# Two transfer queues, a folded scale and filler matmuls in the set-up of an adaLN block with linear attention and experts

## The reference

```python
mod = (silu(c) @ wmod).reshape(2, 6, 1, 256)        # sa, ca, ga, sb, cb, gb
h = layernorm(x) * (1 + ca) + sa
q, k, v = heads(h @ W_qkv)                          # 16 heads of 16
q, k = rope(q), rope(k)
qf, kf = elu(q * 16 ** -0.5) + 1, elu(k) + 1
out = (qf @ (kf.T @ v)) / max(qf @ sum(kf), 1e-6)   # per head
x = x + gate(ga) * (out @ W_out)
h = layernorm(x) * (1 + cb) + sb
x = x + gate(gb) * experts(h)                       # 8 experts, the best 2, capacity 640
```

## Time and profile before

| | us |
|---|---|
| median of 3 runs | 652.75 |
| lowest and highest | 652.57, 653.78 |
| span of the profiled execution | 649.3 |
| around that span, if the execution took the median | 3.45 |
| TensorE, matmuls, busy | 558.4 |
| VectorE, ScalarE, GpSimd busy | 456.7, 318.3, 270.2 |

### The profile page before, as it was taken

The page is one execution under the profiler, slowest core; times in us unless marked ns, Lnnn a source line. Parts: engine busy times, 40 slices in busy tenths (PEclk is TensorE's granted clock), DMA queues, the critical chain, the costliest instruction groups (busy, mean ns, idle before and its releaser), DMA issues.

```text
span 649.3 us, 13329 instructions
## 1 busy us (share of the span) xinstructions
PE 558.4 (86%) x3857; PEld 517.9 (80%) x3857; DVE 456.7 (70%) x1261; ACT 318.3 (49%) x716; POOL 270.2 (42%) x428
## 2 busy tenths in 40 slices
PE   4999889999899510279999999999999999999992
PEld 3677678898777300169999999999999999999992
DVE  3577879998677888877667677577676776666441
ACT  3678768887444410034544544445445444455330
POOL 6588756776678500212107035052070160431221
PEclk9999989999899755579999999999999999999997
DMA  5322258744566560051716627337257175360321
GB/s 164 100 65 69 72 146 257 232 140 142 164 190 194 177 164 1 17 163 34 196 50 124 195 54 156 110 90 158 68 108 209 27 132 160 84 137 10 33 25 16
DMA packets 91910, 75.23 MB, mean 116 GB/s; under 512 B 12108, under 2 KB 88278, under 8 KB 91864
## 3 DMA queue, kind: packets, MB, share of 16 engines
q1 hardware_dynamic: 82872, 58.77, 30.5%
q0 software_dynamic: 8992, 15.90, 13.3%
HBM read 52.48 MB, written 22.16 MB: 115 GB/s over the span
## 4 chain that ended last, share of the span: by engine, by line
PE 57%; DVE 15%; issue 5%; DMA 4%; POOL 2%; ACT 2%; SPq 1%; DVEq 1%; POOLq 0%; ACTq 0%
PE bank L1379 28%; PE bank L1393 14%; PE bank L1414 4%; DVE hit L907 3%; PE bank L1291 2%; PE bank L1428 2%; PE bank L1194 1%; DVE x L870 1%; PE bank L1355 1%; DMA x_in<-x 1%; DMA w_raw<-wd 1%; DVE st L872 1%; PE bank L1336 1%; PE bank L1271 1%; DMA xg<-h_rows,g_idx 1%
## 5 line engine op out<-in xcount | busy, mean ns | idle before, releaser
L508 POOL DMA_INDIRECT xg<-h_rows,g_idx x40 | 44.0, 1100 | 246.3 <-DVE g_idx L1013 236.6
L1379 PE MATMUL bank<-xT_h,w_h 128*128 128x320 f32 x448 | 140.3, 313 | 1.5 <-DVE xT_l L1042 1.0
L1379 PE MATMUL bank<-xT_h,w_l 128*128 128x320 f32 x448 | 138.6, 309 | 0.0
L1379 PE MATMUL bank<-xT_l,w_h 128*128 128x320 f32 x448 | 138.6, 309 | 0.0
L662 ACT CAST hid_h<-hid 128x320 fp32r<-128x320 f32 x112 | 51.5, 460 | 87.6 <-DVE hid L1070 87.6
L518 POOL DMA_INDIRECT out<-yo,s_idx x40 | 67.4, 1685 | 60.7 <-DVE yo L1060 21.9
L1379 PEld LDWEIGHTS bank<-xT_h,w_h 128*128 128x128 f32 x448 | 84.8, 189 | 2.5 <-issue 1.7
L1379 PEld LDWEIGHTS bank<-xT_l,w_h 128*128 128x128 f32 x448 | 84.7, 189 | 0.0
L1379 PEld LDWEIGHTS bank<-xT_h,w_l 128*128 128x128 f32 x448 | 84.6, 189 | 0.0
L658 ACT ACTIVATE act_g<-bank 128x320 f32<-128x320 f32 x112 | 48.9, 437 | 69.4 <-PE bank L1379 68.6
L1075 DVE TENSOR_TENSOR hid_l<-hid,hid_h 128x320 fp32r<-128x320 f32 x112 | 54.8, 489 | 36.6 <-ACT hid_h L662 36.2
(11 more groups left out here) (197 smaller groups left out, 1276.9 us busy)
## 6 DMA issues: line engine op xcount, KB each, us to landing
w_raw<-wg SPq DMA_DIRECT2D x32, 256.0 KB, 3.7
w_raw<-wu SPq DMA_DIRECT2D x32, 256.0 KB, 4.9
w_raw<-wd SPq DMA_DIRECT2D x16, 512.0 KB, 5.9
x_in<-x SPq DMA_DIRECT2D x32, 128.0 KB, 2.1
q_store<-qT SPq DMA_DIRECT2D x32, 128.0 KB, 2.0
q_in<-q_store SPq DMA_DIRECT2D x32, 128.0 KB, 2.1
x_re<-x SPq DMA_DIRECT2D x32, 128.0 KB, 2.1
out<-x SPq DMA_DIRECT2D x32, 128.0 KB, 2.0
```

The costliest lines, as they stand in the source:

```text
L508: nc.gpsimd.indirect_dma_start(out=xg[par][:, a, :], out_offset=None, in_=h2_rows, in_offset=bass.IndirectOffsetOnAxis(ap=g_idx[par][:, a: ...
L1379: last = MM(bank[2 * h + m][:, 0:HCAP], W[i][:, f, at:at + P], XT[j][:, k, cols], start=n == 0, stop=n == 3 * KC - 1)
```

## The change

- SyncE's queue now carries c, the identity alone, x of tiles 0 and 1, the V part of the QKV weights, the rotation table and the other constants. ScalarE's queue carries the modulation weights and the Q and K part, as its first two instructions.
- ScalarE waits for c alone, takes silu, and then the exponential of one number (`warm`), whose result nobody reads.
- The factor 1/4 of Q is taken in ScalarE's rounding and in VectorE's subtraction; the pass over the weights is gone. Rounding and subtraction go in thirds: Q, K, V. The modulation columns are copied behind Q. V is rounded behind tile 0's hT_h and subtracted at the end of step -1. The first product waits for the low parts of Q and K alone, the V product for the third.
- The 90 memsets of `digits` and `swaps` move behind the token loop.
- `keep_warm(n)` multiplies a 128 by 128 tile of ones with itself n times, in bf16, into a bank that nobody has begun to use. TensorE does so 14 times before the transposes of c, 8 times before it waits for the modulation weights, and 24 times before it waits for the low parts ahead of the first product.

The diff, with lines of context left out:

```diff
--- before.py
+++ after.py
@@ -42,6 +42,7 @@
 LAG = TB + 2
+Q_SCALE = float(HD) ** -0.5
 LN_EPS, DEN_EPS, TOPW_EPS, GATE_MIN = 1e-5, 1e-6, 1e-6, 0.25
@@ -174,6 +175,7 @@
         iota_s = sb("iota_s", [P, P], BF16)
+        warm = sb("warm", [1, 1])
@@ -283,6 +285,7 @@
         ld_c, ld_mod, ld_const, ld_w = sem("ld_c"), sem("ld_mod"), sem("ld_const"), sem("ld_w")
+        ld_id, ld_wv, ld_blk = sem("ld_id"), sem("ld_wv"), sem("ld_blk")
         ld_rest, st_mod, ld_ga, ld_all = sem("ld_rest"), sem("st_mod"), sem("ld_ga"), sem("ld_all")
@@ -313,19 +316,21 @@
+        wm = wmod.rearrange("(c p) n -> p c n", p=P)
+        wq = w_qkv.rearrange("(c p) n -> p c n", p=P)
...
         block = ctx.enter_context(nc.Block())
...
             sp.dma_start(c_sb[:, :], c).then_inc(ld_c, 16)
-            sp.dma_start(const_sb[:, :], consts).then_inc(ld_c, 16)
+            sp.dma_start(ident, consts[:, 0:P]).then_inc(ld_id, 16)
             sp.dma_start(x_in[0][:, :], xt[0]).then_inc(ld_x[0], 16)
             sp.dma_start(x_in[1][:, :], xt[1]).then_inc(ld_x[1], 16)
-            wm = wmod.rearrange("(c p) n -> p c n", p=P)
-            sp.dma_start(wmod_sb[:, :, 0:2 * D], wm[:, :, 0:2 * D]).then_inc(ld_mod, 16)
-            sp.dma_start(wqkv_sb[:, :, :], w_qkv.rearrange("(c p) n -> p c n", p=P)).then_inc(ld_w, 16)
+            sp.dma_start(wqkv_sb[:, :, 2 * D:], wq[:, :, 2 * D:]).then_inc(ld_wv, 16)
             sp.dma_start(rope_sb[:, :, :], rope.rearrange("(n p) d -> p n d", p=P)).then_inc(ld_const, 16)
+            sp.dma_start(const_sb[:, P:], consts[:, P:]).then_inc(ld_blk, 16)
@@ -444,13 +449,6 @@
                            allow_small_or_imprecise_dtypes=True).then_inc(plink_s, 1)
-            for n in range(DIGITS):
-                unit = 1 << (TOP_BIT - 1 - 2 * n)
-                for d in range(3):
-                    nc.gpsimd.memset(digits[:, n, d:d + 1], (d + 1) * unit)
-                    ins = nc.gpsimd.memset(swaps[:, n, d:d + 1], (d + 1) * unit | ((d + 1) * unit >> 2))
-            ins.then_inc(plink_s, 1)
...
             def step(s):
@@ -497,7 +495,12 @@
+            for n in range(DIGITS):
+                unit = 1 << (TOP_BIT - 1 - 2 * n)
+                for d in range(3):
+                    nc.gpsimd.memset(digits[:, n, d:d + 1], (d + 1) * unit)
+                    ins = nc.gpsimd.memset(swaps[:, n, d:d + 1], (d + 1) * unit | ((d + 1) * unit >> 2))
+            ins.then_inc(plink_s, 1)
             pool.wait_ge(lgc, NT)
@@ -545,8 +548,12 @@
         def _(act):
-            act.wait_ge(ld_c, 32)
+            act.dma_start(wmod_sb[:, :, 0:2 * D], wm[:, :, 0:2 * D]).then_inc(ld_mod, 16)
+            act.dma_start(wqkv_sb[:, :, 0:2 * D], wq[:, :, 0:2 * D]).then_inc(ld_w, 16)
+            act.wait_ge(ld_c, 16)
             nc.scalar.activation(c_act[:, :], c_sb[:, :], ACT.Silu).then_inc(act_pre, 1)
+            act.wait_ge(plink_s, 1)
+            nc.scalar.activation(warm[:, :], half_neg[0:1, :], ACT.Exp)
@@ -563,13 +570,14 @@
                 if s.rep == -1:
-                    act.wait_ge(dve_pre, 2)
-                    nc.scalar.copy(wqkv_h[:, :, 0:2 * D], wqkv_sb[:, :, 0:2 * D]).then_inc(act_pre, 1)
-                    nc.scalar.copy(wqkv_h[:, :, 2 * D:], wqkv_sb[:, :, 2 * D:]).then_inc(act_pre, 1)
+                    act.wait_ge(ld_w, 16)
+                    nc.scalar.activation(wqkv_h[:, :, 0:D], wqkv_sb[:, :, 0:D], ACT.Copy, scale=Q_SCALE)\
+                        .then_inc(act_pre, 1)
+                    nc.scalar.copy(wqkv_h[:, :, D:2 * D], wqkv_sb[:, :, D:2 * D]).then_inc(act_pre, 1)
                 if on["trh"]:
...
                     if s.rep == -1:
-                        act.wait_ge(dve_pre, 4)
+                        act.wait_ge(dve_pre, 3)
                     wait(act, tr_h, s.t(2))
@@ -585,6 +593,9 @@
                     nc.scalar.copy(hT_h[s.par(1)][:, :, :], hT[:, :, :]).then_inc(hTh_d, 1)
+                if s.rep == -1:
+                    act.wait_ge(ld_wv, 16)
+                    nc.scalar.copy(wqkv_h[:, :, 2 * D:], wqkv_sb[:, :, 2 * D:]).then_inc(act_pre, 1)
                 if on["kv"]:
@@ -712,6 +723,12 @@
+            def w_low(i):
...
+                sl = slice(i * D, (i + 1) * D)
+                dve.wait_ge(act_pre, 2 + i)
+                return V.tensor_tensor(wqkv_l[:, :, sl], wqkv_sb[:, :, sl], wqkv_h[:, :, sl].bitcast(F32), ALU.subtract)
...
             def mod_rows(part):
@@ -720,6 +737,7 @@
                     V.tensor_scalar(mod_row[:, 2, :], row_ps[1][:, 0:D], 1.0, None, ALU.add)
+                    dve.wait_ge(ld_blk, 16)
                     V.tensor_copy(same_e[:, :], same_f)
@@ -782,7 +800,7 @@
                 link(TT(hot1, q, b8(first), ALU.is_equal))
-                dve.wait_ge(act_pre, 4 + part)
+                dve.wait_ge(act_pre, 5 + part)
                 link(V.scalar_tensor_tensor(rest, hot1, -2.0, ex, ALU.mult, ALU.add))
@@ -800,17 +818,11 @@
                 if s.rep == -1:
-                    dve.wait_ge(ld_w, 16)
-                    V.tensor_scalar(wqkv_sb[:, :, 0:D], wqkv_sb[:, :, 0:D], float(HD) ** -0.5, None, ALU.mult)\
-                        .then_inc(dve_pre, 1)
-                if s.rep == -1:
-                    for i, sl in enumerate((slice(0, 2 * D), slice(2 * D, 3 * D))):
-                        dve.wait_ge(act_pre, 2 + i)
-                        ins = V.tensor_tensor(wqkv_l[:, :, sl], wqkv_sb[:, :, sl], wqkv_h[:, :, sl].bitcast(F32),
-                                              ALU.subtract)
-                        if i == 0:
-                            mod_cols()
-                    ins.then_inc(dve_pre, 1)
+                    dve.wait_ge(act_pre, 2)
+                    V.scalar_tensor_tensor(wqkv_l[:, :, 0:D], wqkv_sb[:, :, 0:D], Q_SCALE, wqkv_h[:, :, 0:D].bitcast(F32),
+                                           ALU.mult, ALU.subtract)
+                    mod_cols()
+                    w_low(1).then_inc(dve_pre, 1)
                 if s.rep in (LAG, NT - 4):
@@ -844,6 +856,8 @@
                     finish_stats(mv1, nm1[s.par(3)], ve1[s.par(3)], ag1, stat1, s.t(4))
+                if s.rep == -1:
+                    w_low(2).then_inc(dve_pre, 1)
                 if on["feat"]:
@@ -873,7 +887,7 @@
                 if s.rep == NT + LAG:
-                    dve.wait_ge(plink_s, 13)
+                    dve.wait_ge(plink_s, 12)
                     choose(0, EARLY)
@@ -902,6 +916,7 @@
             link(V.tensor_copy(valT[:, :], bank[0][:, 0:2 * P]))
+            dve.wait_ge(plink_s, 13)
             for n in range(DIGITS):
@@ -1172,11 +1187,20 @@
             PASSES = ((0, 0), (0, 1), (1, 0))
+            def keep_warm(n):
...
+                for _ in range(n):
+                    MM(bank[3][:, 0:P], ones_b[:, :], ones_b[:, :], start=True, stop=True)
...
+            pe.wait_ge(plink_s, 2)
+            keep_warm(14)
             pe.wait_ge(act_pre, 1)
+            pe.wait_ge(ld_id, 16)
             for k in range(KC):
...
             pe.wait_ge(dve_pre, 1)
+            keep_warm(8)
             pe.wait_ge(ld_mod, 16)
@@ -1217,7 +1241,8 @@
                     if s.rep == 0:
-                        pe.wait_ge(dve_pre, 5)
+                        keep_warm(24)
+                        pe.wait_ge(dve_pre, 4)
                     wait(pe, hTl_d, s.t(1))
@@ -1232,6 +1257,8 @@
                     wait(pe, v_done, s.t(0))
+                    if s.rep == 0:
+                        pe.wait_ge(dve_pre, 5)
                     product(v_ps, (hT_h[s.par(0)], hT_l[s.par(0)]), (wqkv_h, wqkv_l), slice(2 * D, 3 * D))\
...
```

## The result

The change made the kernel slower. On one chip the changed kernel took 655.32 us (median of 20 runs, 652.26 to 661.73) beside 653.27 us for the kernel before (20 runs): a ratio of 1.0039, 95% interval 1.0022 to 1.0056. Two more sets on other occasions gave 1.0040 (1.0023 to 1.0057) and 1.0040 (1.0027 to 1.0053). That is 2.0 to 2.7 us lost where I had forecast 1.95 us gained. The single runs scatter by several microseconds, and the long ones show a lower mean granted clock of TensorE (0.941 in the shortest of the 20, 0.931 in the longest), so what follows rests on ratios and on places in the trace that come back in every execution. The changed kernel's profiled execution took 654.88 us, with a span of 652.6.

What follows compares the result with a forecast made beforehand. The prediction took the set-up up to tile 0's first rotation (17.55 us) as what counts, with TensorE busiest at 86%. Rotation at 16.0 gains 1.55, plus 0.4 from the table load: 1.95, so 650.8 us, range 647.7 to 652.9.

Steps and rivals of the forecast that it cites:

- Edits at nothing: Moved memsets fill GpSimd's 2.49 us idle before the reset, pushing it back 0.5; new waits and split constants also cost nothing.
- The 24 ones: On TensorE ahead of the first product: start at 14.1 instead of 11.9, costing 2.2 us at half speed, 0.8 at full.
- near the fast end: First product to rotation of tile 0: 1.9 us taken, between 1.71 at full speed and 3.01 at half.
- my early bound: Earliest landing of the modulation weights on ScalarE's queue: issue at 0.75 plus 4.7 us, so 5.45.
- GpSimd has hn by then: Set-up, before tile 0's transposes end at 9.97: hn is ready because the 90 memsets no longer delay GpSimd's first step.
- the table load at 22.16: ScalarE's 1.28 us load moves to about 3.4 through the small exponential; only about 0.4 us can be gained.
- The second-queue rival: Modulation weights on ScalarE's queue still land at 7.3; only the table load gains, giving 652.2 us; chance 20%.
- the late end: Slow end of the forecast's own range, with landing at 6.8 and product at 3.0 us: 652.4 us.
- The 3.45 us around the span: Median whole time 652.75 lies 3.45 above the profiled span 649.3; the same was added to the new span.
- The early ones: The 14 and 8 ones on TensorE end at 5.5, before the modulation weights land, and cost nothing; 0.5 if weights came at 5.0.
- After it nothing waits for a fixed moment: Behind tile 0's first rotation at 17.55 us: whatever brings that rotation forward comes off the kernel's end.

Runs made afterwards that it cites:

- e8: The changed kernel once more, unchanged, timed against the kernel before: ratio 1.0040.
- e3: The changed kernel without any of the 46 products of ones, memsets still moved: ratio 0.9972 to the kernel before.
- e4: The changed kernel without the products of ones and with the memsets back ahead of GpSimd's token loop: ratio 0.9957, on a second occasion 0.9963.
- e2: The kernel before with only the 90 memsets moved behind GpSimd's token loop: ratio 1.0020, 1.3 us slower.
- e1: The changed kernel with only the 90 memsets put back ahead of GpSimd's token loop: ratio 1.0005 to the kernel before.
- the corners: Four kernels on one chip, f1 to f4: memsets moved or back, 24 ones in or out; the move cost 0.37% with the ones, 0.35% without.
- f1: The changed kernel as it is, with moved memsets and all 46 ones, timed beside f2, f3 and f4: ratio 1.0040.
- f3: The changed kernel without the 24 ones, memsets still moved, the 14 and 8 kept; the 24 ones cost f1 0.23% against it.
- f2: The changed kernel with memsets back ahead of the loop and all 46 ones kept, same program as e1; the move cost f1 0.37% against it.
- f4: The changed kernel with the memsets back and the 24 ones out, the 14 and 8 kept, same program as e6: ratio 0.9982.
- e6: The kernel of e1 without the 24 ones ahead of tile 0's product, the 14 and 8 kept: ratio 0.9982 to the kernel before.
- e7: The kernel of e4 with 46 one-column products of ones added behind TensorE's token loop: ratio 0.9983 to the kernel before.
- e11: The kernel of e1 with the 24 ones replaced by 8 behind tile 0's transposes and 5 behind tile 1's: ratio 0.9951, 646.72 us.
- g1: The kernel of e11 timed once more, unchanged: ratio 0.9939 to the kernel before.

## Why the prediction was wrong

**The step "Edits at nothing" failed, and with it the sign.** I costed the moved memsets at nothing, because they fill GpSimd's idle time ahead of the reset. That idle time was real, and the reset moved by 0.25 us, less than the 0.5 I allowed. The step asked who waits for the memsets and not what they share with an engine that is working. VectorE was choosing experts in the 2.6 us of the memsets and was held up by 1.5: the short instruction took 1.96 to 2.42 us in all six executions with the move and 0.18 in the others. In five it ended within 0.04 us of the last of the 90; in e8 it ended at 225.22, when the reset's first memset, which followed them at 224.67 without a pause, was over. The Trainium skill, SBUF — State Buffer, section "Who interferes with whom", says that VectorE and GpSimd share a pair of ports, that a tensor_scalar can need the pair and is then blocked by a GpSimd instruction that holds it, and that an operation on two tensors is not blocked by one that only writes. The traces agree on both, with L809 at 1.96 us and L808 at its usual 0.37; that it is the ports is not shown by a run. The page speaks of one instruction holding the pair, and here a row of 0.09 us memsets kept VectorE waiting until the row was over. It was the page to weigh in the prediction, and I weighed another. The traces show 1.5 us for the move (1.3 to 2.0 by pair). The ratios price it at 1.0 (e3 against e4), 1.3 (e2), 2.2 (the changed kernel against e1), 2.3 and 2.4 us (the corners), so the noise may be all of the difference. An untested rival is the clock: the runs of f1 and f3 had a mean granted clock of 0.937 and 0.936, those of f2 and f4 about 0.939 each, and e3 and e4, with the smallest price, 0.938 both.

**The step "The 24 ones" was right in its place and wrong in its weight.** I put the product's start at 14.1 with them and 11.9 without; it was 14.37 to 14.75 in five executions with them and 12.74 to 13.25 in the eleven without 128-column ones there. So the delay was foreseen, 2.2 us by my sum and 1.6 where x landed alike; the ones took what I had said, and it was the product without them that I had put 0.8 to 1.4 us too early. Its repayment was not. I took 1.9 us from the product's start to the rotation, "near the fast end"; the five with the 24 took 2.31, 2.86, 2.59, 2.41 and 2.12 us, mean 2.46, and six without them 3.01 each. The 24 bought 0.55 us and cost 1.6, and the rotation came about 1 us later than it would have. I also had the comparison in hand and never made it: 11.9 + 3.01 = 14.9 without the ones, 14.1 + 1.9 = 16.0 with them. By my own prices they lose, even at the fast end (14.1 + 1.71 = 15.8).

**What was right in the set-up, and what only looked so.** L1185's successor took its 3.52 at half speed, as forecast, and started at 6.27 (forecast 5.9). The weights themselves had landed at 4.5 (issued at 0.75, 3.8 us to landing), earlier than my early bound, and what held TensorE was the identity until 4.84 and then the 8 ones. So a start near 5.9 was partly luck. L1216's successor ran from 9.86 to 10.55; my sum had it end at 9.97. **The step "GpSimd has hn by then" failed**: I left the landing of x where it was, and with ScalarE's two transfers issued ahead of it, it moved from 4.06 to 6.84 us. The first statistics ran at 6.86 in place of 4.68, and hn was done at 9.80, as late as the sixteen products. Without ones ahead of these, in e4, the transposes waited 0.49 us for hn. hT then ended at 11.46 where I had 10.85, and hT_l at 12.93 where my sum has 11.9: VectorE took the statistics of a later tile (11.87 to 12.30) before it. That is 1 us of the forecast gain. The QK weights landed by 6.49, and the table load at 22.16 is gone. It brought more than the 0.4 I gave it: from the first rotation to that of tile 3 took 13.1 us in both executions of the kernel before and 12.5 in all three of the changed one. The second-queue rival is refuted: the modulation products start at 6.27, and at 5.47 where no ones stand ahead of them, not at 7.3. Of the 2.7 us by which their weights land earlier (4.50 for 7.22), 1.8 is the earlier issue; the price was x.

One sum of the forecast was off in itself. Landing at 6.8 and product at 3.0 put the rotation at 18.0, which gives 652.8 as the late end and not 652.4. The 3.45 us around the span also stands for two different executions: in the runs that list both, the whole time lies 1.8 to 3.0 us above the span. Neither changes the account.

**The early ones cost nothing, as forecast.** The 8 stood ahead of a product whose weights were there and moved it by 0.8 us (5.47 to 6.27), but the transposes of tile 0 wait for hn until 9.54 in any case. With them and without them, beside 13 later ones: 0.9939 and 0.9938. Without those the picture is less clean: 0.9982 twice with the 14 and the 8 (e6, f4), 0.9957 and 0.9963 with no ones, and nothing in the set-up to account for it but x's landing.

**"After it nothing waits for a fixed moment" failed.** I had put the opposite among what would prove me wrong, and it did. The set-up itself brought less than my 1.95: in the first pair of profiles 0.66 at tile 0 and 1.26 from tile 3 on, where the missing table load has its effect; over all executions the rotation of tile 0 came at 17.15 on average of three with the changed kernel and 17.3 of two with the kernel before.

**The sum as measured.** Two queues, folded scale, columns first and early tables, with no 24 ones and memsets at the start: between -0.2% with 14 and 8 ones in place and -0.4% without, so 1.2 to 2.8 us gained. The 24 ones +1.4 to 1.5, the memsets +2.3 to 2.4. With the corner f4 that is -1.2 + 1.4 + 2.4 = +2.6 us, and the changed kernel stands at +0.40%, 2.6 us. The corners add up to it by their making, so this sum proves nothing. The places in the traces give less: 0.15 us gained at the rotation and 0.6 by the table load, 1.5 lost at the search, so a loss of 0.8 us; the other 1.8 us have no place. The parts that gain were put too high as well: without the 24 my own terms give 17.55 - 14.9 + 0.4 = 3.05 us, and the ratios 1.2 with the 14 and 8 and 2.4 to 2.8 with no ones. But it was the two parts costed at or below nothing that turned the sign.

**What stays open.** Theory B, the longer program, is neither shown nor refuted as a cost of its own. TensorE's 46 extra instructions elsewhere (e7) may have cost 1 us; 35 extra in e11 and g1 went with the fastest times of all. f4 and e6, one program, both gave 0.9982, and the addition of 13 ones that fit gave 0.9951 and 0.9939; 0.5 us of this lies on the way to the search (14.3 in place of 13.8) and 0.1 to 0.4 at the rotation, with x's landing; the rest has no place. Nor is it explained why 48 ones cost 2.3 us at the rotation and no more than 0.9 at the end, or why runs of one program differ in their granted clock.

## What to carry to other kernels

An engine's idle time is a free place for work only if the work shares nothing with the engines that are busy then: before moving a run of small GpSimd instructions, look at what VectorE does in that stretch, and ask whether it is the one that sets the end. When a transfer is brought forward, look for the one that lands later for it, and whether it is now the start of the chain. Filler work on TensorE belongs where it ends before the next input comes; compare start-without plus slow product to start-with plus fast product before adding any. And a change with several parts wants its parts priced apart: here a gain of up to 0.4% was buried under two edits that looked free.

## What the hardware did that was not expected

- 90 memsets of 128x1 on GpSimd, 0.09 us each, held a VectorE TENSOR_SCALAR of 128x26 for 1.96 to 2.42 us where it takes 0.18, in six executions out of six. Ahead of the token loop, where VectorE mostly waited for transfers, the same memsets cost nothing that a run could show (rotation 16.83 with them there, 16.89 without). A TENSOR_SCALAR of 128x1 ran among them there in its usual time, in the kernel before:

```profile
5.45 0.15 DVE L752 TENSOR_SCALAR nm<-mv 128x1 f32<-128x1 f32 x1
```

- The moment at which TensorE's spacing quickens at the start of a program is not fixed by the program. It lay at about 15.7 and behind 16.5 in two executions of one program without any ones, and at about 15.2, 15.7, 15.9, 16.3 and 17.2 in five with all 46; with one-column ones the product stayed slow to its end at 17.05. The granted-clock column reads 1.00 throughout, as it did in the earlier trace rows.
- A DMA issue of SyncE that takes 0.4 us took 1.0 to 2.1 us 52 times in 20 profiles (20 to 216 us), and each time a 16 KB block of instructions was being fetched; of 4055 shorter issues 126 overlap such a fetch. No run changed the fetches by themselves, so which causes which is not tested.
- With the modulation and QK weights issued first on ScalarE's queue, x of tile 0, issued on SyncE's at the same 1.59 us as before, landed at 6.51 to 7.02 us in place of 4.01 to 4.06.
